# Two heads to a PSUM bank in an attention kernel's narrow steps, and head copies ahead of the step's item

## What is computed

```python
q, k, v = (xn @ W.T for W in (Wq, Wk, Wv))      # 16 heads of 8, q and k rotated (RoPE)
scores = einsum('bqhd,bkhd->bhqk', q, k) / sqrt(8), -inf above the diagonal
out = softmax(scores) @ v, heads joined, @ Wo.T
probs = softmax(x_flat @ router_w.T)            # 8 experts, the best 2, weights normalised
y = relu(x @ w1[e].T + b1[e]) @ w2[e].T + b2[e] # hidden width 512
```

## Time and profile before

| what | value |
|---|---|
| median of 3 runs | 774.55 us (770.61 to 775.82) |
| the profiled execution | 773.38 us, its span 771.6 us |
| mean granted TensorE clock of it | 0.958 |
| instructions in the span | 19063 |

### The profile page before, as it was taken

The page is one execution under the profiler, slowest core; times in us unless marked ns, Lnnn a source line. Parts: engine busy times, 40 slices in busy tenths (PEclk is TensorE's granted clock), DMA queues, the critical chain, the costliest instruction groups (busy, mean ns, idle before and its releaser), DMA issues. The chain is left out here.

```text
span 771.6 us, 19063 instructions
## 1 busy us (share of the span) xinstructions
PE 715.4 (93%) x6544; PEld 420.0 (54%) x6544; DVE 574.9 (75%) x977; ACT 457.2 (59%) x1090; POOL 255.5 (33%) x306
## 2 busy tenths in 40 slices
PE   9899898999999999999999997999999989989897
PEld 3465343544544544544444445999999934343344
DVE  6956988788788788788788784666666659878344
ACT  3544025667677677676676675666666637647451
POOL 2566111523433423333324331000000057556651
PEclk9899999999999999999999998999999979979599
DMA  8599840337356235135144041322222361211644
GB/s 219 136 226 236 259 63 16 54 67 123 79 87 131 58 62 79 34 56 77 29 64 73 23 73 53 96 68 68 68 67 68 88 113 42 54 32 41 155 124 135
DMA packets 64623, 69.40 MB, mean 90 GB/s; under 512 B 9934, under 2 KB 52430, under 8 KB 64490
## 3 DMA queue, kind: packets, MB, share of 16 engines
q1 hardware_dynamic: 60458, 60.08, 35.5%
q0 software_dynamic: 4096, 8.40, 4.2%
HBM read 41.11 MB, written 26.67 MB: 88 GB/s over the span
## 5 line engine op out<-in xcount | busy, mean ns | idle before, releaser
L737 ACT ACTIVATE probs<-bank 128x512 f32<-128x512 f32 (+3 forms) x768 | 326.1, 492 | 209.3 <-PE bank L1223 202.9
L845 DVE TENSOR_REDUCE mx<-bank 128x2 f32<-128x1024 f32 (+3 forms) x320 | 348.1, 1115 | 84.4 <-PE bank L1206 67.6
L1223 PE MATMUL bank<-stack 64*128 64x512 f32 (+3 forms) x768 | 210.5, 445 | 18.9 <-ACT probs L737 18.3
L637 POOL TENSOR_SCALAR_AFFINE_SELECT probs<-probs 128x512 f32<-128x512 f32 x128 | 81.8, 640 | 432.3 <-ACT probs L737 276.9
L1257 PE MATMUL bank<-probs,vst 128*32 128x256 f32 (+3 forms) x2304 | 193.9, 410 | 5.2 <-POOL probs L637 2.9
L1223 PEld LDWEIGHTS bank<-stack 64*128 64x128 f32 x768 | 94.0, 190 | 181.6 <-ACT probs L737 135.7
L1199 PE MATMUL bank<-stack 64*128 64x512 f32 (+3 forms) x768 | 163.6, 384 | 4.4 <-DVE mx L845 4.4
L1199 PEld LDWEIGHTS bank<-stack 64*128 64x128 f32 x768 | 83.7, 192 | 13.7 <-DVE mx L845 11.1
L1301 PE MATMUL bank<-tiles_s,staged 128*128 128x128 f32 x576 | 79.6, 282 | 0.7 <-ACT tiles_s L742 0.7
L1257 PEld LDWEIGHTS bank<-probs,vst 128*32 128x32 f32 x2304 | 46.4, 110 | 58.9 <-ACT probs L737 19.4
L1319 PE MATMUL bank<-staged,q_high 128*128 128x128 f32 x576 | 76.6, 276 | 0.5 <-DVE k_high L1027 0.5
(11 more groups left out here) (131 smaller groups left out, 447.5 us busy)
## 6 DMA issues: line engine op xcount, KB each, us to landing
stack<-parts_d SPq DMA_DIRECT2D x96, 128.0 KB
slots_in_d<-const_s SPq DMA_DIRECT2D x4, 1152.0 KB, 9.0
tiles_s<-slots_in_d SPq DMA_DIRECT2D x72, 64.0 KB, 1.8
slots_out_d<-k_high SPq DMA_DIRECT2D x72, 64.0 KB, 1.6
early<-in_w_experts SPq DMA_DIRECT2D x8, 514.0 KB, 5.3
stack<-parts_d SPq DMA_DIRECT2D x64, 64.0 KB
parts_d<-probs SPq DMA_DIRECT2D x8, 512.0 KB, 6.1
heads_d<-xnT SPq DMA_DIRECT2D x124, 18.0 KB
```

Of the source, the lines that this page charges most:

```text
L637: pool.affine_select(out=t, in_=t, compare_op=ALU.is_ge, fill=0.0, base=0, pattern=[[0, HG], [1, P]], channel_multiplier=-1).then_inc(s["d ...
L737: nc.scalar.activation(probs[n % 3][:, h, q0:HALF], st_of(at)[:, 0:HALF - q0], ACT.Exp, scale=SCALE).then_inc(s["probs_made"], 1)
L845: v.tensor_reduce(to, src.rearrange("p g (a k) -> p g a k", k=w), AX_X, ALU.max, negate=True).then_inc(s["scores_read"], 1)
L1223: mm(st_of(at)[:, 0:HALF - q0], kstk[r][g][:, hp, kb * P:(kb + 1) * P], qstk[r][g][:, hp, c * HALF + q0:(c + 1) * HALF], start=True, stop=True
```

## The change

It has four parts. (1) In the steps of at most 256 columns (`SHARED`: steps 2, 3, 10 and 11) the scores of two heads go side by side into one PSUM bank, heads 0 and 2 to the first and 1 and 3 to the second, and ScalarE has one exponential for each bank. Counts of semaphores go by banks, 40 a unit (`NB`, `banks_before`). Where such a step is scored, all four heads stand ahead of the first products. (2) `in_two` no longer asks for kb > 0, so the products of steps 0 and 4 are divided into two halves as well; the second half's first matmul doesn't have the start flag. (3) VectorE copies the heads of steps 3 and 11 (`HEADS_AT`) before it reads the step's item, not after. (4) TensorE makes that step's item behind the scores of the next two steps' last heads, after the first products.

```diff
+        SHARED = [HALF - q0 <= HALF // 2 for _, _, q0 in STEPS]
+        BANKS = [2 if shared else HG for shared in SHARED]
+        NB = sum(BANKS)
+        def banks_before(u, n):
+            return u * NB + sum(BANKS[:n])
...
+        def st_of(u, n, i):
+            return st[(banks_before(u, n) + i) % 3]
+        HEADS_AT = [3, NS - 1]
...
-                    for h in range(HG):
-                        at = n * HG + h
-                        act.wait_ge(s["scoresT_made"], u * (NS * HG) + at + 1)
-                        nc.scalar.activation(probs[n % 3][:, h, q0:HALF], st_of(at)[:, 0:HALF - q0], ACT.Exp,
-                                             scale=SCALE).then_inc(s["probs_made"], 1)
+                    for i in range(BANKS[n]):
+                        act.wait_ge(s["scoresT_made"], banks_before(u, n) + i + 1)
+                        if SHARED[n]:
+                            to = probs[n % 3][:, i::2, q0:HALF]
+                            src = st_of(u, n, i)[:, 0:2 * (HALF - q0)].rearrange("p (h q) -> p h q", h=2)
+                        else:
+                            to, src = probs[n % 3][:, i, q0:HALF], st_of(u, n, i)[:, 0:HALF - q0]
+                        nc.scalar.activation(to, src, ACT.Exp, scale=SCALE).then_inc(s["probs_made"], 1)
...
                 for j in range(NS):
+                    if j in HEADS_AT:
+                        heads_out(u, HEADS_AT.index(j))
                     for ahead, n in plan_of(u, j):
...
-                    if j == 3:
-                        heads_out(u, 0)
-                    if j == NS - 1:
-                        heads_out(u, 1)
...
+                i, col = (g, hp * (HALF - q0)) if SHARED[n] else (h, 0)
+                at = banks_before(u, n) + i
+                if col == 0 and at >= 3:
+                    pe.wait_ge(s["probs_made"], at - 2)
+                made = mm(st_of(u, n, i)[:, col:col + HALF - q0], kstk[r][g][:, hp, kb * P:(kb + 1) * P],
+                          qstk[r][g][:, hp, c * HALF + q0:(c + 1) * HALF], start=True, stop=True)
+                if not SHARED[n] or hp == PAIRS - 1:
+                    made.then_inc(s["scoresT_made"], 1)
...
-                return kb > 0 and q0 <= P
+                return q0 <= P
...
-                              start=kb == 0, stop=kb == 4 * c + 3)
+                              start=kb == 0 and begin == 0, stop=kb == 4 * c + 3)
...
-                    for h in range(HG):
-                        if more(u, ahead):
-                            score(u + ahead, (r + ahead) % 4, n, h)
-                        if h % 2 and todo:
+                    if SHARED[n]:
+                        both = [range(HG), ()]
+                    else:
+                        both = [range(2), range(2, HG)]
+                    for i, heads in enumerate(both):
+                        for h in heads:
+                            if more(u, ahead):
+                                score(u + ahead, (r + ahead) % 4, n, h)
+                        if todo and j not in HEADS_AT:
                             score_item(*todo.pop(0))
-                        if h == 1:
+                        if i == 0:
                             first_products(u, r, j)
```

More of the change, by code:

```diff
@@ L326, in share_of @@
             return range(before, before + table[r][i])
-        def st_of(n):
-            return st[n % 3]
+        def st_of(u, n, i):
+            return st[(banks_before(u, n) + i) % 3]
+        HEADS_AT = [3, NS - 1]
         def gather_order(n):
@@ L416, in unit @@
                     if past(u):
-                        sp.wait_ge(s["scoresT_made"], u * (NS * HG))
+                        sp.wait_ge(s["scoresT_made"], banks_before(u, 0))
                     load_stacks(u + 3, (r + 3) % 4)
@@ L632, in unit @@
                     if kb >= 4 * c:
-                        pool.wait_ge(s["probs_made"], (u * NS + n + 1) * HG)
+                        pool.wait_ge(s["probs_made"], banks_before(u, n + 1))
                         pool.sem_inc(s["diag_seen"], 1)
@@ L1218, in score @@
                 c, kb, q0 = STEPS[n]
-                at = n * HG + h
-                if not (isinstance(u, int) and u * NS * HG + at < 3):
-                    pe.wait_ge(s["probs_made"], u * (NS * HG) + at - 2)
                 hp, g = divmod(h, 2)
-                mm(st_of(at)[:, 0:HALF - q0], kstk[r][g][:, hp, kb * P:(kb + 1) * P],
-                   qstk[r][g][:, hp, c * HALF + q0:(c + 1) * HALF], start=True, stop=True
-                   ).then_inc(s["scoresT_made"], 1)
+                i, col = (g, hp * (HALF - q0)) if SHARED[n] else (h, 0)
[6 more added lines that the diff above has]
+                    made.then_inc(s["scoresT_made"], 1)
             def first_products(u, r, n):
@@ L1233, in first_products @@
                     pe.wait_ge(s["heads_copied"], 2 * u + c)
-                pe.wait_ge(s["probs_made"], u * (NS * HG) + (n + 1) * HG)
+                pe.wait_ge(s["probs_made"], banks_before(u, n + 1))
                 if kb >= 4 * c:
@@ L1389, in _ @@
             pe.wait_ge(s["heads_copied"], 2 * UNITS)
-            pe.wait_ge(s["probs_made"], UNITS * NS * HG)
+            pe.wait_ge(s["probs_made"], banks_before(UNITS, 0))
             mm(st[0], sum_rows, oraw[1], start=True, stop=True).then_inc(s["sums_spread"], 1)
```

## The result

The changed kernel takes 747.73 us (median of 4 executions, 746.91 to 760.36) against 774.09 for the kernel before: ratio 0.9696, 95% interval 0.9640 to 0.9752. The profiled execution took 747.16 us, its span 745.4.

The account below looks back on a forecast made before the run. TensorE, busy 93% of the span and waiting for ScalarE before scores, was taken as the bound. Eleven steady units at 0.65 (7.2 us) plus 2.0 elsewhere gave 9.2 off the 774.55 median: 765 us, range 754 to 776.

Parts of the forecast that it names:

- A: Steady unit from score (step 0, head 2) to step 0's products: 3.79 us becomes 3.61, a gain of 0.18.
- B: Steady unit from step 0's products to score (step 4, head 0): 4.05 us becomes 3.96, a gain of 0.09.
- C: Steady unit from score (step 4, head 0) to step 5's products: 8.21 us now, a gain of 0.44.
- ScalarE's row of eight: Steps 2 to 4: eight back-to-back exponentials of 512 columns, 4.26 us, 0.53 each, starting as now and holding a waiting score.
- taking the item out of the way gains 0.06 and no more: Step 3's products move up, but score (6,1) stays held by exponential (5,2) until 4.65 us, now 4.71.
- The deduction from 0.71 to 0.65 a unit: Steady-unit gain of 0.71 us taken as 0.65 because VectorE's reads never come closer than its 1.1 to 1.2 rhythm.
- Its saving alone is worth nothing: Steps 2, 3, 10, 11: fewer ScalarE exponentials gain nothing, since ScalarE is busy 224 of 324 us.
- estimated 0.2 us: Per unit, worth of eight fewer semaphore increments at about 26 ns each by the skill's rule; left out of the sum.
- The first and last units, 0.4 each and 2.0 in all: First unit and last four gain 0.4 us each, 2.0 together, given their extra items, combining and gathers.
- a rival, at 4 us and two places: Step 4's products at 665.45 and 37.5 us later: head-copy waits and clock falls may vanish, 4 us; chance 2 in 10.
- All waits go: Rival: every wait goes and the end keeps its clock, about 755 us (758 to 751); chance 2 in 10.
- Only the order changes: Rival: holds return one score later, a unit gains 0 to 0.3, about 772 us; 3 in 10, including sharing doing nothing.
- fall of the clock in steady units: Rival: short waits from step 10 to step 0 lower the clock, costing 1.7 us a unit, about 784; 0.7 in 10.

Follow-up runs that it names:

- u_no_heads: Changed kernel with head copies again behind the item's read and the item again before the products: 758.59 us, ratio 0.984 to the kernel before.
- dve_only: Changed kernel with TensorE's item again before the products of steps 3 and 11, VectorE's head copies still early: 754.47 us, a single execution.
- after_again: The changed kernel without any edit, six more executions: 758.67 us, ratio 0.968 to the kernel before.
- b_fill: Kernel before, with scores of steps 9 and 6 issued again in TensorE's waits in the last four units: 767.09 us, ratio 0.994.
- a_fill: Changed kernel with scores issued again in TensorE's waits, in the first and last four units: 744.88 us, ratio 0.962 to the kernel before.
- pe_only: Changed kernel with VectorE's head copies again behind the item's read, TensorE's order as changed: 780.69 us, a single execution.

## Why the prediction was wrong, point by point

The sum had two terms, 7.2 us for the eleven steady units and 2.0 us for the first and last ones; everything else stood at nothing. In the profiled pair they came to 10.1 and 16.1. So 3 us of the miss lie in the steady units and 14 outside them, and of these 14 about 8 are clock and 5 to 6 are schedule.

- *The steady unit.* Right in mechanism, short in size. A was 3.63 for 3.61. B gained 0.17 for 0.09: the item alone behind products took 0.53 (264.10 to 264.63), where 0.59 had been chosen between 0.47 and 0.64. C gained 0.61 for 0.44.
- *The step of C that failed* is "ScalarE's row of eight [...] 0.53 each". 4.26 / 8 = 0.53 was read as the pace of a chain that nothing could shorten, and "taking the item out of the way gains 0.06 and no more" followed. After, the same eight take 4.03; where the item is put back (u_no_heads, dve_only) they take 4.25 again. The row held one gap, in front of the fifth exponential and too short to be shown as idle, in which ScalarE waited for score (5,2), which stood behind the item. The head order was worth 0.22 there (5.36 against 5.14 to step 4's products), and 0.27 from step 10 to step 0 (3.90 without it, from 261.00 to 264.90 in u_no_heads, against 3.63).
- *The deduction from 0.71 to 0.65 a unit* had no row behind it but VectorE's rhythm, which the gain did not meet; measured 0.92. Over eleven units 7.2 was forecast and 10.1 came.
- *Sharing.* "Its saving alone is worth nothing" was right, and shown by undoing it. With sharing go eight increments a unit too, and 28.55 with it against 28.53 without shows no trace of the estimated 0.2 us that the rule of the Trainium skill (TensorE: Matmul & The Clock Gate, "The cost: per-tile semaphore tail") would give them. It rightly stayed out of the sum.
- *The first and last units, 0.4 each and 2.0 in all,* are the term that failed most. At equal clock the change is worth 17 to 18 us, of which 10.1 are the eleven units; the other 7 to 8 lie in the rest, which had been given 2.0. At the clock of before the last stretch gained 2.7 us (124.14 for 126.82), where the four units had been given 1.6. Rows at full clock on both sides show some of it: unit 13 from the copy at 654.67 to the one at 664.72 took 10.05 and now 9.36, the last unit's second half 22.30 and now 20.75 (21.32 in after_again). The experts with unit 12's start, which were to change nothing, took 163.8, and 160.5 and 161.1 in the two traces of the changed kernel. No run takes the 7 to 8 us further apart, so the step that failed is known and its cause in part open.
- *The clock.* The sum put it at nothing; it stood in a rival, at 4 us and two places. In the profiled pair it gave about 8. b_fill shows that this loss is real in the kernel before and shrinks when TensorE's waits are filled with work. That the change itself lowers the loss is not shown: over all executions it went from 32.3 to 29.9, and in after_again the changed kernel fell as the kernel before does. So part of the 26 us is the luck of the first four executions, three of them at a clock of 0.970 to 0.972; the median of all ten, 755.5 us, lies inside the range that the first four missed. That is no merit of the sum either: it is still 18 us below the kernel before, twice the 9 forecast.
- *The rivals.* "All waits go" came nearest (1.22 us of recorded waits a unit were named; the total went from 18.3 to 6.0). The measured time lies below even its 751, and by its own terms, 4 us and 10 to 13 off 774.55, it should have read 761 to 758. "Only the order changes" is refuted by the additive 0.51 and 0.45, though its side case, that sharing does nothing, came true. The fall of the clock in steady units did not come: 1.00 over 314 us.

## What to carry to other kernels

A merged row of n instructions divided by n is an upper bound of the pace, from one start to the next, that they could keep: before a chain is called unshortenable, look into the row for a short gap, or compare it with the same instructions in a stretch where nothing feeds them late. Two reorderings on two engines can be worth 0.5 us a unit together, nothing with VectorE's half alone and minus 1.6 with TensorE's alone (30.63 against 29.03; minus 1.35 at full clock), so walk both queues past the moved instruction. Where the granted clock differs between executions, put each time beside its clock, and compare stretches of like clock, before saying what a change gave. Filling TensorE's long waits with repeated matmuls paid in both kernels; more of them than a_fill has cost 2 us and gave nothing.

## What the runs showed of the hardware that was not expected

- One and the same kernel lost between 20.8 and 38.0 us of clock from execution to execution, and its time went with it, 745.0 to 762.6 us. Even steady units are not safe: those of b_fill are the unchanged ones of the kernel before, which ran at 1.00 in its trace, and yet the clock was at its lower level from 274.3 to 277.7 us; pe_only's had one such fall too, from 309.2 to 316.0. Each us lost cost 0.68 to 0.75 us of time by the fits above.
- Matmuls added to waits made a kernel faster: by 7 us between medians in the kernel before (767.1 against 774.0; 0.6% by the ratio), and in a_fill by 3 us against the changed kernel's first four executions (744.9 against 747.7) and 14 against its six further ones.
- The Trainium skill (TensorE: Matmul & The Clock Gate, "HAM oscillation — how this bites in real kernels") tells of a kernel in which idle gaps of TensorE, longer ones than any named here, bring its clock down again and again. Here unit 13's turn waited 1.75 us and the clock fell from 679 on in the kernel before, and from 666 on in one execution of the changed kernel; in another the same wait was passed at 1.00 (from 651.66 to 673.05). So the length of that wait alone does not decide it, and what tips it from one execution to the next stays open.
